# A 32-image, seven-stage pipeline of four residual blocks on one core: setup shared out among the engines, last steps reordered, VectorE's list shortened, two channel masks made by ScalarE

## The chip, the core and the metric

The kernel runs on one core of a Trainium2 chip. The core has five engines with a queue of instructions each: TensorE (PE in the profile; PEld is its loading of weights), VectorE (DVE), ScalarE (ACT), GpSimd (POOL) and SyncE (SP), which here only issues transfers. The engines wait for each other through semaphores. The metric is device time in microseconds (us) of one execution; lower is better.

## The reference, cut to what matters

The input `x` has 32 images of 256 channels and 28 by 28 pixels. Four blocks follow one another, each of them `x = x + block(groupnorm(x))`, with 32 groups of 8 channels:

```
pooled = x.mean(axis=(2, 3)); g = sparsemax(pooled @ gate_w.T + gate_b)
out = einsum('boi,bihw->bohw', einsum('bk,koi->boi', g, expert_w), x)
...
h = prune(relu(bn(depthwise3x3(x) + dw_b)), 4.0)
out = prune(relu(bn(conv1x1(h) + pw_b)), 0.001)
...
q, k, v = split(xt @ Wqkv + bqkv); q = q - mean(q); k = k - mean(k)
k2n = normed(k*k / sum(k*k)) over tokens; q2n = normed(q*q / sum(q*q)) over channels
out = (v + q2n @ (k2n.T @ v) / sqrt(784)) @ Wln + bln
...
out = box3x3(x) / 9
```

`prune` sets a whole channel of an image to zero where its largest value is under the threshold. Since the values come out of a ReLU, "largest value at least the threshold" is the same as "the sum of relu(value - just under the threshold) is above zero". That sum is `h_over` or `y_over`, and the 0 or 1 of each channel is `hmask` or `ymask`.

## The kernel before, in words

The 256 channels are two halves (`j` or `J` = 2) of 128 partitions with 784 columns. The images go through seven stages, and each step `t` (from -1 to 36) works on seven neighbouring images at once: Z = t+1 is loaded, squared and split into a high and a low part; A = t goes through the gate (`gate_logits`, `sparsemax`), the mix of experts (`mix_experts`, `scaled_mix`, `mixed_low`) and the first convolution (`mixed_conv`, `make_x1`); B = t-1 through the depthwise convolution (`first_tap` on ScalarE, then 16 taps of `depthwise` on VectorE, eight per half); C_ = t-2 through the masks and the pointwise convolution (`relu_h`, `sum_over_h`, `h_high`, `h_low`, `pointwise`, `relu_y`, `sum_over_y`, `make_x2`); D = t-3 through the squares of queries and keys and their norms (`square_k`, `square_q`, `fourth_powers_q`, `q_norms`, `q_scales`, `scale_q`, `keys_x`, `kx_low`); E = t-4 through the attention output (`key_rows`, `key_norms`, `value_out`, `attention_out`, `make_x3`); F = t-5 through the box filter. For most images the box is two row sums on VectorE (`box_row_sums`) and three accumulating transfers issued by GpSimd (`add_rows`); for the last two images (TAIL, "in_tail") it is ten additions on VectorE (`box_in_tail`) and a store.

A stage is left out where its image does not exist, so the first steps (images come in) and the last ones (from t = 32, where A is gone) do only part of the work. Steps 8 to 29 are a loop of two steps each; the others are written out.

Each engine's order is the order of the calls in its own `step` (PE L663, DVE L1031, ACT L1328, POOL L1455); nothing else schedules. A step begins with one matmul that makes the group means of all four layers (`group_means`, L488, at the end of PE's list); VectorE reads them (`gn_avg`, L780), makes variances (L786), ScalarE takes the roots (L1114), VectorE makes `gn_r` and `gn_s` (L792, L794) and then the rows `k_rows` (L967). PE has `value_out` of half 0, then waits for these rows in `key_norms` (L540).

Setup: VectorE centres the bias row of queries and keys and splits it in three (L724 to L734) before its first `gn_avg`, does the folded batch-norm constants and the query and key weights at t = 0 (L743 to L756, `parts_of` L715), and the other weights at the end of t = 1 (`setup_weights`, L715 to L772). PE has the weight products at t = 1 (`setup`, L444 to L455).

The two masks are VectorE's, L869 and L883:

```
dve.wait_ge(h_over_sum.sem, h_over_sum.at(C_))
nc.vector.tensor_scalar(hmask[:], h_over[:], 0.0, None, ALU.is_gt).then_inc(hmask_step.sem, 1)
```

## Time and profile before

| what | us |
|---|---|
| median of 3 executions | 1546.27 (1545.89 to 1547.4) |
| the profiled execution, its own time | 1547.11 |
| its span, first to last instruction | 1545.4 |
| PE busy, matmuls | 1404.6 (91%) |
| DVE busy | 1389.4 (90%) |
| ACT busy | 1277.0 (83%) |
| POOL busy | 312.1 (20%) |
| steps 5 to 31, 27 of them, from group means to group means | 1188.14, or 44.01 each |
| from the first instruction to the fourth step's group means (t = -1 to 2) | 107.8 |
| steps 32 to 36 | 161.9 |

The granted clock is TensorE's: 1.00 in the tables is 2.4 GHz and 0.50 is 1.2 GHz, and a stretch with both has a value between. The profile's row of slices shows it at full speed through nearly all of the span, and lower in the first four slices and at the end. A time read from a timeline row is the start of that group and how long it lasted; what stands in brackets is how long the engine was idle before, and what ended that.

### The profile page before, as it was taken

What the parts mean: (1) busy time and instruction counts of PE and PEld (TensorE: products, weight loads), DVE (VectorE), ACT (ScalarE), POOL (GpSimd) and SP (SyncE); (2) the same over time, 40 slices, a digit from 0 to 9 for tenths busy, and PEclk for the clock granted to TensorE, in tenths of its full rate; (3) what the DMA queues carried; (4) which work ended last, traced back from release to release, by engine and by line L of the source; (5) the groups of instructions that cost most, each with busy time, mean ns of one, the idle gap of its engine ahead of it and who ended that gap; (6) DMA issues with size and microseconds to landing.
All of it is one profiled execution on the core that took longest, in us unless ns stands there. A gap on an engine that the chain in (4) does not pass through costs nothing. (4 is left out here: it accounts for less than half of the span.)

```text
span 1545.4 us, 28737 instructions
## 1 busy us (share of the span) xinstructions
PE 1404.6 (91%) x9538; PEld 1246.2 (81%) x9538; DVE 1389.4 (90%) x2553; ACT 1277.0 (83%) x2569; POOL 312.1 (20%) x232
## 2 busy tenths in 40 slices
PE   3449999999999999999999999999999999999983
PEld 2338988888889888888888888888888888888872
DVE  5788899999999999999999999999999999998547
ACT  3268898888899988888999888889998888987852
POOL 2220112222222121211221122212212222111000
PEclk9769999999999999999999999999999999999987
DMA  4100134434443444344443433444434344344431
GB/s 136 41 21 22 38 69 95 94 85 86 103 104 85 81 97 90 84 91 94 104 88 78 101 86 86 99 85 104 93 73 104 83 91 97 64 84 84 84 63 42
DMA packets 45575, 127.92 MB, mean 83 GB/s; under 512 B 3793, under 2 KB 4817, under 8 KB 45522
## 3 DMA queue, kind: packets, MB, share of 16 engines
q0 software_dynamic: 24480, 72.26, 28.1%
q1 hardware_dynamic: 20946, 54.99, 10.2%
q8 instruction: 29, 0.48, 0.1%
q14 instruction: 24, 0.20, 0.0%
q10 hardware_dynamic: 96, 0.00, 0.0%
HBM read 29.29 MB, written 97.94 MB: 82 GB/s over the span
## 5 line engine op out<-in xcount | busy, mean ns | idle before, releaser
L862 DVE SCALAR_TENSOR_TENSOR h<-xpad,dw_sb,h 128x784 f32<-128x784 f32 x512 | 493.6, 1031 | 0.0
L659 PE MATMUL tile_ps<-k,xT 112*128 112x256 f32 x896 | 204.7, 387 | 0.0
L659 PEld LDWEIGHTS tile_ps<-k,xT 112*128 112x128 f32 x896 | 171.6, 194 | 23.1
L585 PE MATMUL tile_ps<-wqk,xn_parts 128*112 128x256 f32 x1344 | 187.5, 294 | 0.0
L1429 POOL TENSOR_SCALAR xpad<-x,gn_rs 128x784 f32<-128x784 f32 x64 | 87.5, 1373 | 483.3 <-DVE x L921 461.4
L1453 POOL DMA_DIRECT2D out<-row_sums x90 | 108.0, 1200 | 364.7 <-DMA out<-row_sums 216.4
L1440 POOL TENSOR_TENSOR x_parts<-x,x_parts 128x784 fp32r<-128x784 f32 x64 | 112.3, 1772 | 339.3 <-ACT x_parts L1180 339.3
L1120 ACT ACTIVATE junk<-x 128x784 bf16<-128x784 f32 x192 | 163.5, 860 | 15.2 <-DVE x L887 4.8
L585 PEld LDWEIGHTS tile_ps<-wqk,xn_parts 128*112 128x112 f32 x1344 | 170.1, 176 | 0.1
L646 PE MATMUL conv_ps<-x_parts,mixed_parts 128*128 128x392 f32 (+1 forms) x768 | 150.6, 353 | 7.4 <-DVE mixed_parts L901 7.4
L504 PE MATMUL conv_ps<-xn_parts,w_out 128*128 128x392 f32 x768 | 152.3, 347 | 0.0
L646 PEld LDWEIGHTS conv_ps<-x_parts,mixed_parts 128*128 128x128 f32 x768 | 140.9, 194 | 10.2 <-issue 10.2
L504 PE MATMUL conv_ps<-hq_parts,pw_parts 128*128 128x392 f32 x768 | 146.1, 346 | 0.0
L504 PE MATMUL conv_ps<-xn_parts,wqk 128*128 128x392 f32 x768 | 142.6, 341 | 0.0
L504 PE MATMUL conv_ps<-hq_parts,attn_parts 128*128 128x392 f32 x768 | 142.4, 341 | 0.0
L504 PEld LDWEIGHTS conv_ps<-hq_parts,pw_parts 128*128 128x128 f32 x768 | 136.4, 189 | 1.7 <-DVE hq_parts L875 1.7
L504 PEld LDWEIGHTS conv_ps<-hq_parts,attn_parts 128*128 128x128 f32 x768 | 137.2, 188 | 0.4 <-DVE attn_parts L980 0.4
L504 PEld LDWEIGHTS conv_ps<-xn_parts,wqk 128*128 128x128 f32 x768 | 135.6, 188 | 0.0
L504 PEld LDWEIGHTS conv_ps<-xn_parts,w_out 128*128 128x128 f32 x768 | 133.4, 188 | 0.0
L1199 ACT ACTIVATE xT<-tile_ps,k_rec 112x256 f32<-112x256 f32 x224 | 89.4, 525 | 0.3 <-PE tile_ps L518 0.3
L1294 ACT ACTIVATE k<-tile_ps 112x256 f32<-112x256 f32 x224 | 83.2, 390 | 4.2 <-PE tile_ps L585 4.2
L631 PE MATMUL small_ps<-expert_sb,mix_w 128*32 128x512 f32 x512 | 66.7, 641 | 8.2 <-DVE mix_w L851 8.2
(162 smaller groups left out, 2748.0 us busy)
## 6 DMA issues: line engine op xcount, KB each, us to landing
out<-row_sums POOLq DMA_DIRECT2D x90, 784.0 KB, 7.1
x<-x SPq DMA_DIRECT2D x32, 784.0 KB, 4.4
out<-x SPq DMA_DIRECT2D x30, 784.0 KB, 3.5
expert_sb<-expert_rows SPq DMA_DIRECT2D x8, 256.0 KB, 5.1
out<-x SPq DMA_DIRECT2D x4, 392.0 KB, 2.4
x<-w_qk SPq DMA_DIRECT2D x1, 512.0 KB, 3.8
x<-w_vT SPq DMA_DIRECT2D x1, 256.0 KB, 7.5
x<-w_ln SPq DMA_DIRECT2D x1, 256.0 KB, 7.5
```

The lines of the kernel that those rows point to most:

```text
L504: mm = nc.tensor.matmul(conv_ps[:, 2 * j + a, 0:HALF], wt[:, half(j)], act[:, a * HALF:(a + 1) * HALF], start=(first and i == 0), stop=(la ...
L585: mm = nc.tensor.matmul(dst, xn2_parts[:, u, i, m * TOK:(m + 1) * TOK], wqk[:, v, i, C:2 * C], start=False, stop=(i == J - 1 and u == 1))
L631: mm = nc.tensor.matmul(small_ps[s * SUB:(s + 1) * SUB, :], mix_w[:, g, :], expert_sb[:, g, s, :], start=(g == 0), stop=(g == PACKED - 1), ...
L646: mm = nc.tensor.matmul(conv_ps[:, 2 * j + a, 0:width], mixed_parts[:, u, i * C + j * P:i * C + (j + 1) * P], x0_parts[:, v, i, a * HALF:a ...
L659: mm = nc.tensor.matmul(tile_ps[:, KX_BANK, i * C:(i + 1) * C], xT[:, m, half(i)], k2[:, m, :], start=(m == 0), stop=(m == M - 1))
L862: nc.vector.scalar_tensor_tensor(acc, view, scalar, acc, ALU.mult, ALU.add).then_inc(dw_step[j].sem, 1)
L1120: nc.scalar.activation(junk[:, j * HW:(j + 1) * HW], source[:, j, :], ACT.Square, accum_out=gn_in[:, layer, 2 + j:3 + j]).then_inc(gn_sums ...
L1199: nc.scalar.activation(xT[:, m, :], tile_ps[0:TOK, XT_BANK[m // 2], m % 2 * C:(m % 2 + 1) * C], ACT.Identity, scale=k_rec[:, m:m + 1]).the ...
L1294: nc.scalar.activation(k2[:, m, :], tile_ps[0:TOK, K_BANK[m // 2], m % 2 * C:(m % 2 + 1) * C], ACT.Square, accum_out=k_sum[:, m:m + 1]).th ...
L1429: nc.gpsimd.tensor_scalar(xpad[:, j, 1:1 + H, 1:1 + W], x1[:, B.odd, j, :].rearrange("p (h w) -> p h w", w=W), gn_r[:, 1, j:j + 1], gn_s[: ...
L1440: nc.gpsimd.tensor_tensor(x0_parts[:, 1, j, 0:HW], x0[:, Z.odd, j, :], x0_parts[:, 0, j, 0:HW].bitcast(F32), ALU.subtract).then_inc(x0_lo. ...
L1453: pool.dma_start(out_dram[F.times(1)], rows, accum_op=ALU.add).then_inc(rows_added[n].of(F), 16)
```

## The change

All of it is order or place of small instructions; no large one is added or taken away.

1. **Masks.** `hmask` and `ymask` are made by ScalarE, as Sign of the two sums, directly behind `sum_over_h` and `sum_over_y`. VectorE's two comparisons go.
2. **VectorE's list, each step.** The sparsemax is written by ranks (two instructions fewer, one reduction over twice the elements); `box_scale` and `mean_lows` go to GpSimd; the square of `k_rec` goes to ScalarE; the limit on the query norm is folded into the two instructions behind the reciprocal; the first gate product is made between variance and reciprocal (`centred_sums`). GpSimd's `normalise_x1` waits for `xn2_lo` in place of `x3_ready`.
3. **Setup.** The bias row is centred and split by ScalarE and GpSimd; ScalarE does the query and key weights at t = 0 but for their low part; PE makes the output weights at t = 0 and VectorE splits them there. The rest of the setup is made at t = 2. ScalarE has its first tap ahead of the sums at t = 1 and 2, and VectorE takes three taps ahead of `mixed_low` there and, at t = 1, seven behind `make_x1`. The first activation is a Sqrt in place of a Square.
4. **Last steps.** Where A is gone, each half of the queries is squared twice at once, the sums of fourth powers go to another PSUM bank and stand ahead of the second half of `pointwise`, and VectorE takes 8 taps ahead of `q_scales`. In the last two steps the box additions of image 30 stand between the other instructions, and `normalise_x3` of a tail image comes early.

```
@@ VectorE, each step
+            def centred_sums(A):
+                dve.wait_ge(gn_read.sem, gn_read.at(A))
+                nc.vector.scalar_tensor_tensor(pooled[:, 0, :], gn_in[:, 0, 0:2], 1.0 / HW, gn_avg[:, 0, 0:2], ALU.mult,
+                                               ALU.subtract).then_inc(gate_step.sem, 1)
...
-                nc.vector.tensor_scalar(zz[:, 1], zz[:, 0], 0.0, None, ALU.max).then_inc(s.sem, 1)
+                nc.vector.tensor_tensor(zz[:, 1], zz[:, 0], z[:].unsqueeze(1).to_broadcast([P, EXPERTS, EXPERTS]),
+                                        ALU.mult).then_inc(s.sem, 1)
...
-                nc.vector.tensor_reduce(excess[:], zz[:, 1], AX.X, ALU.add).then_inc(s.sem, 1)
+                nc.vector.tensor_reduce(upper[:, 0:2, :], zz[:], AX.X, ALU.add).then_inc(s.sem, 1)
...
             def q_scales(D):
                 dve.wait_ge(q_root.sem, q_root.at(D))
-                nc.vector.tensor_scalar(q_alpha[:, 0, :], q_norm[:], NORM_EPS * DIV_EPS, float(HW) ** 0.5, ALU.max,
-                                        ALU.mult).then_inc(alpha_step.sem, 1)
...
+                nc.vector.reciprocal(q_alpha[:], q_norm[:]).then_inc(alpha_step.sem, 1)
...
+                nc.vector.tensor_scalar(alpha_cut, q_alpha[:], ALPHA_MOST, low_row, ALU.min, ALU.mult).then_inc(alpha_step.sem, 1)
@@ ScalarE, the masks
+            def h_mask(C_):
+                act.wait_ge(h_over_sum.sem, h_over_sum.at(C_))
+                if (C_ - 1).active:
+                    act.wait_ge(h_lo.sem, h_lo.at(C_ - 1))
+                nc.scalar.activation(hmask[:], h_over[:], ACT.Sign).then_inc(hmask_step.sem, 1)
+            def y_mask(C_):
...
+                nc.scalar.activation(ymask[:], y_over[:], ACT.Sign).then_inc(ymask_step.sem, 1)
@@ ScalarE, step
+                if F.in_tail:
+                    normalise_x3(F)
...
                 if C_.active:
                     sum_over_h(C_, 0)
                     sum_over_h(C_, 1)
+                    h_mask(C_)
                     h_high(C_)
...
-                if D.active:
-                    square_q(D)
+                if D.active and A.active:
+                    for j in range(J):
+                        square_q(D, j)
                     copy_tokens(D, range(6))
-                    fourth_powers_q(D)
+                    for j in range(J):
+                        fourth_powers_q(D, j)
+                elif D.active:
+                    for j in range(J):
+                        square_q(D, j)
+                        fourth_powers_q(D, j)
+                    copy_tokens(D, range(3))
                 if C_.active:
                     relu_y(C_, 0)
+                    if A.active:
+                        sum_over_y(C_, 0)
+                if D.active:
+                    q_norms(A, D)
+                    if not A.active:
+                        copy_tokens(D, range(3, 6))
+                if C_.active and not A.active:
                     sum_over_y(C_, 0)
-                if D.active:
-                    q_norms(D)
                 if C_.active:
                     relu_y(C_, 1)
                     sum_over_y(C_, 1)
+                    y_mask(C_)
                 if D.active:
                     copy_tokens(D, range(6, M))
                     fourth_powers(D)
@@ TensorE, step
+                if t.number == 0:
+                    setup_output()
                 if D.active:
                     keys(D)
                     queries(D)
                     x2_to_tokens(D, range(3))
                 if C_.active:
-                    pointwise(C_, range(2))
+                    pointwise(C_, range(2 if A.active else 1))
                 if D.active:
-                    query_sums(D)
+                    query_sums(A, D)
+                if C_.active and not A.active:
+                    pointwise(C_, range(1, 2))
@@ VectorE, step
                 if F.in_tail:
-                    box_in_tail(F)
+                    box_in_tail(F, range(5, 7) if E.active else range(10))
                 elif F.active:
                     box_row_sums(F)
+                early = 3 if t.number in (1, 2) else 0
+                if B.active:
+                    depthwise(B, slice(0, early))
...
+                late = 9 if t.number == 1 else 11 if A.active else 8
@@ GpSimd, step
+                if F.active:
+                    box_scale(A, F)
+                if A.active:
+                    mean_lows(A)
+                if t.number == 0:
+                    setup_bias()
                 if B.active:
-                    normalise_x1(A, B, C_, E)
+                    normalise_x1(A, B, C_, D, E)
```

The order of VectorE's instructions in the first full depthwise step (t = 1), before, from the experts' weights on: `mix_w` is the gate's last result, `h<-xpad` are taps, `x,gn_in<-conv_ps` is `make_x1`.

```order
L851 SCALAR_TENSOR_TENSOR mix_w<-gate_own,zeros,mix_const 128x64
L893 TENSOR_TENSOR x_parts<-gn_avg,x_parts 128x2x2
L901 SCALAR_TENSOR_TENSOR mixed_parts<-small_ps,gn_rs,mixed_parts 128x256 x2
L862 SCALAR_TENSOR_TENSOR h<-xpad,dw_sb,h 128x784 x11
L911 SCALAR_TENSOR_TENSOR x,gn_in<-conv_ps,x 128x784 x2
L862 SCALAR_TENSOR_TENSOR h<-xpad,dw_sb,h 128x784 x5
L715 CAST pw_parts<-x 128x512
L716 TENSOR_TENSOR pw_parts<-x,pw_parts 128x512
L715 CAST w_out<-tile_ps 128x512
L716 TENSOR_TENSOR w_out<-tile_ps,w_out 128x512
```

And of the change, the same place, up to the next group means:

```order
L858 SCALAR_TENSOR_TENSOR mix_w<-gate_own,zeros,mix_const 128x64
L869 SCALAR_TENSOR_TENSOR h<-xpad,dw_sb,h 128x784 x3
L893 SCALAR_TENSOR_TENSOR mixed_parts<-small_ps,gn_rs,mixed_parts 128x256 x2
L869 SCALAR_TENSOR_TENSOR h<-xpad,dw_sb,h 128x784 x6
L903 SCALAR_TENSOR_TENSOR x,gn_in<-conv_ps,x 128x784 x2
L869 SCALAR_TENSOR_TENSOR h<-xpad,dw_sb,h 128x784 x7
L793 COPY gn_avg<-small_ps 128x16
```

Three taps now stand ahead of `mixed_low`, and no weight is split in this step.

ScalarE's order in an ordinary step, before, from the roots of the query sums to the last fourth power:

```order
L1319 ACTIVATE q_norm<-tile_ps 128x196
L1284 ACTIVATE x<-conv_ps,bn_shift,bn_scale 128x784
L1276 ACTIVATE over,y_over<-x,below 128x784
L1199 ACTIVATE xT<-tile_ps,k_rec 112x256
L1219 ACTIVATE fourth<-k 112x1792
```

And of the change:

```order
L1371 ACTIVATE q_norm<-tile_ps 128x196
L1338 ACTIVATE x<-conv_ps,bn_shift,bn_scale 128x784
L1330 ACTIVATE over,y_over<-x,below 128x784
L1312 ACTIVATE ymask<-y_over 128x2
L1235 ACTIVATE xT<-tile_ps,k_rec 112x256
L1257 ACTIVATE k_rec<-k_rec 112x7
L1259 ACTIVATE fourth<-k 112x1792
```

The mask of `y` stands between its sum and the next copy, and the square of `k_rec` ahead of the fourth powers; the mask of `h` stands in the same way between its sums and `h_high`.

VectorE's order in step 35, before, from the attention weights on; `row_sums`, `x3pad` and `x<-x,x3pad` are the box additions of image 30:

```order
L980 SCALAR_TENSOR_TENSOR attn_parts<-tile_ps,k_inv,attn_parts 128x256 x2
L921 SCALAR_TENSOR_TENSOR x,gn_in<-conv_ps,b_out,x 128x784 x2
L935 TENSOR_TENSOR row_sums<-x3pad 128x784
L937 TENSOR_TENSOR row_sums<-row_sums,x3pad 128x784
L940 TENSOR_TENSOR x3pad<-row_sums 128x28x28
```

And of the change:

```order
L936 TENSOR_TENSOR row_sums<-x3pad 128x784
L972 SCALAR_TENSOR_TENSOR attn_parts<-tile_ps,k_inv,attn_parts 128x256 x2
L936 TENSOR_TENSOR row_sums<-row_sums,x3pad 128x784
L936 TENSOR_TENSOR x3pad<-row_sums 128x28x28
L913 SCALAR_TENSOR_TENSOR x,gn_in<-conv_ps,b_out,x 128x784
L936 TENSOR_TENSOR x3pad<-x3pad,row_sums 128x28x28
L936 TENSOR_TENSOR x<-x,x3pad 128x784
L913 SCALAR_TENSOR_TENSOR x,gn_in<-conv_ps,b_out,x 128x784
```

Five additions now stand ahead of the last `make_x3`, and one of them ahead of the low part of the attention weights, for which PE waits.

## Rows read from the trace of the kernel before

**Rows 1.** The page: the span in 40 slices, tenths.

```profile
PE   3449999999999999999999999999999999999983
PEclk9769999999999999999999999999999999999987
```

**Rows 2.** Busy time by stretch: stretch, its length, each engine's busy us (count), clock, DMA.

```profile
core 0: us, PE busy (x) PEld busy (x) DVE busy (x) ACT busy (x) POOL busy (x), PEclk, DMA share, GB/s
14.34:40.21 25.87, 12.01 (x46) 8.62 (x46) 13.79 (x51) 6.59 (x17) 2.88 (x2) 0.87 0.21 65
40.21:77.03 36.82, 15.84 (x70) 12.85 (x70) 27.94 (x55) 8.12 (x18) 8.58 (x5) 0.70 0.09 30
77.03:111.11 34.08, 15.16 (x70) 11.57 (x70) 29.30 (x51) 19.50 (x36) 6.33 (x4) 0.65 0.07 24
111.11:153.09 41.98, 36.62 (x240) 31.03 (x241) 33.67 (x64) 35.52 (x71) 5.37 (x4) 0.86 0.07 20
195.32:1383.46 1188.14, 1159.88 (x8022) 1034.32 (x8020) 1136.87 (x2080) 1068.25 (x2153) 261.55 (x187) 1.00 0.43 90
1426.53:1467.15 40.62, 37.96 (x255) 34.32 (x253) 21.34 (x39) 32.37 (x64) 3.61 (x3) 0.96 0.42 80
1467.15:1508.17 41.02, 35.34 (x231) 31.12 (x229) 17.40 (x31) 21.76 (x46) 3.61 (x3) 0.88 0.36 59
1508.17:1545.40 37.23, 11.26 (x70) 10.78 (x68) 26.73 (x43) 8.10 (x15) 0.00 (x0) 0.70 0.11 44
```

**Rows 3.** Waits in the 27 steps from 195.32 to 1383.46: total, times, longest.

```profile
ACT gn_sd L1114 <- DVE gn_var L786: 37.9, 27, 1.6
PE tile_ps L540 <- DVE k_rows L967: 28.3, 27, 1.2
```

**Rows 4.** Timeline of one ordinary step (start, length): ScalarE's rows, then VectorE's.

```profile
732.07 1.59 ACT L1233 CAST xn_parts<-xn 128x784 fp32r<-128x784 f32 x2 [0.81 <-PE conv_ps L504]
...
737.85 1.79 ACT L1266 ACTIVATE hq_parts<-h,hmask 128x784 fp32r<-128x784 f32 x2 [0.24 <-DVE hmask L869]
...
755.18 0.32 ACT L1319 ACTIVATE q_norm<-tile_ps 128x196 f32<-128x196 f32 x1
...
755.53 0.26 DVE L1004 TENSOR_SCALAR q_alpha<-q_norm 128x196 f32<-128x196 f32 x1
...
757.88 0.16 DVE L883 TENSOR_SCALAR ymask<-y_over 128x2 f32<-128x2 f32 x1
758.08 1.04 DVE L887 SCALAR_TENSOR_TENSOR x<-x,ymask 128x784 f32<-128x784 f32 x1
...
768.62 0.68 DVE L1028 TENSOR_TENSOR kx_parts<-tile_ps,kx_parts 128x512 fp32r<-128x512 f32 x1
```

**Rows 5.** Timeline of the same step: a GpSimd and a VectorE row that overlap.

```profile
736.75 3.60 POOL L1429 TENSOR_SCALAR xpad<-x,gn_rs 128x784 f32<-128x784 f32 x2 [15.64 <-DVE x L921]
...
739.67 2.31 DVE L955 TENSOR_TENSOR row_sums<-row_sums,x3pad 128x1568 f32<-128x1568 f32 x1
```

**Rows 6.** Timeline of the first steps, t = -1 to 1.

```profile
8.77 1.28 ACT L1096 ACT_TABLE_LOAD   x1
...
20.15 3.64 PE L631 MATMUL small_ps<-expert_sb,mix_w 128*32 128x512 f32 x16 [2.74 <-DVE mix_w L851]
...
29.09 7.02 PE L646 MATMUL conv_ps<-x_parts,mixed_parts 128*128 128x392 f32 x24 [5.30 <-DVE mixed_parts L901]
...
53.97 10.49 DVE L862 SCALAR_TENSOR_TENSOR h<-xpad,dw_sb,h 128x784 f32<-128x784 f32 x11
```

**Rows 7.** Timeline of the last steps, t = 33 to 35.

```profile
1456.93 0.69 PE L613 MATMUL tile_ps<-kx_parts,picks 128*128 128x196 f32 x4 [2.66 <-DVE kx_parts L1015]
...
1492.71 1.53 PE L601 MATMUL tile_ps<-fourth,ones 128*32 128x196 f32 x16 [3.37 <-ACT fourth L1312]
...
1498.13 8.26 PE L659 MATMUL tile_ps<-k,xT 112*128 112x256 f32 x28
...
1520.13 0.97 DVE L935 TENSOR_TENSOR row_sums<-x3pad 128x784 f32<-128x784 f32 x1
```

351 lines of the change are left out of this document (204 added, 147 removed).

## The prediction

> **What bounds the kernel now.** I read the slices of the page first [rows 1]: PE is busy nine tenths or more everywhere but in the first four slices and the last ones. So there are three kernels in one: a start (t = -1 to 3), 27 ordinary steps and more like them, and an end (t = 32 to 36). The busy table by stretch gives each its price [rows 2]. An ordinary step takes 1188.14 / 27 = 44.01 us, with PE busy 1159.88 / 27 = 42.96 and DVE 42.11. The missing 1.05 us of PE is one wait, for `k_rows` in front of L540: 28.3 / 27 = 1.05 [rows 3]. VectorE is the late one: ScalarE waits 37.9 / 27 = 1.4 us for its variance [rows 3].
>
> That looks like a VectorE bound, and the change cuts VectorE's list. But the timeline of one step shows a closed chain through three engines [rows 4]. ScalarE's L1233 starts at 732.07 when PE is through with `value_out`; ScalarE then works without a gap worth naming until `q_norm` ends at 755.18 + 0.32 = 755.50, 23.43 later; VectorE starts `q_alpha` on it at 755.53, and from there to the end of `kx_low` at 768.62 + 0.68 = 769.30 it is 13.77 more; then come the means, `k_rows` and PE's next `value_out`, some 6.7, and L1233 again. 23.43 + 0.03 + 13.77 + 6.7 = 43.9, nearly the whole step. VectorE's own list and this chain are within 0.1 us of each other. **What the chain does not lose, the step does not lose.**
>
> **The ordinary steps, part by part.** A small dependent VectorE instruction costs 0.20 from start to start (757.88 to 758.08), an independent one about 0.08 (estimates from these rows) [rows 4].
> - Ahead of `q_alpha` VectorE loses: the `hmask` comparison with its wait 0.4, `k_rec` squared 0.2, the gate's first product 0.2 (its successor lies under the wait for ScalarE's root), the sparsemax about 0.2 net, `box_scale` and `mean_lows` 0.15. About 1.15. In many steps GpSimd's second `xpad` meets the row sums: two halves take 3.60, and L955 takes 2.31 [rows 5]. The new wait lets `xpad` start about 1 us earlier, ahead of them; I allow 0.5. All this, 1.6 us, ends in a wait for `q_norm`, which ScalarE does not bring earlier. In the chain it is worth nothing.
> - Behind `q_alpha`: its first instruction of 0.26 goes, 0.30 with the gap. Behind the two cuts VectorE wants `ymask`. That now comes from ScalarE, one Sign behind a sum that VectorE had reached just before. So `make_x2` starts some 0.2 earlier, not 0.5.
> - ScalarE gets the Sign of `h` in the chain: about 0.2 for a tiny activation plus two hand-overs to itself, 0.35, against the gap of 0.24 for VectorE's comparison [rows 4]: +0.1. Bounds: 0 where the old gap was longer, +0.3 if a Sign costs as much as the 0.32 of `q_norm`. The Sign of `y` and the square of `k_rec` lie behind `q_norm`, where ScalarE has a wait for PE to give up.
> - GpSimd's two small instructions run in its idle time (15.64 before `xpad` [rows 5]); if GpSimd took 2 us for each they would still be ahead of L1143 and of `mixed_conv`.
>
> Sum: -0.2 +0.1 in the chain, and -0.1 for the steps in which VectorE itself was last (the collision). **-0.2 per step, for 28 steps (t = 4 to 31): -5.6.** Bounds: +0.1 (+3) and -1.05 (-29), the whole of PE's wait.
>
> **The start.** VectorE's first group-mean row is at 14.34, where the next stretch begins [rows 2], because the bias row comes ahead of it, and the second table load of 1.28 and its root stand at 8.77 [rows 6]. Without them it follows PE's first matmul at about 9.5: -4.8.
> - t = 0 (25.87 [rows 2]): the gate to `mix_w` needs about 6 us, PE's mix 3.64 [rows 6]. VectorE's query and key weights no longer stand between mix and `mixed_low` (part of the 5.30 before L646), but PE has `setup_output` there, 1.9 to 3.8 by the clock (an estimate: it has a third to a half of the work of L646). L646 then takes its 7.02 [rows 6], and behind it ScalarE has one sum of squares less, 0.95. 9.5 + 6 + 3.6 + 3.8 + 7.0 + 3.1 = 33.0 for the next `gn_avg` against 40.21: -2.4 on top. Hidden under it: ScalarE's bias chain (some 8 us while it waited for PE) and its weights (5 us under L646). If that cover fails, the mix starts up to 3 us later.
> - t = 1 (36.82): 11 taps began at 53.97, behind `mixed_low` [rows 6], and the weights' splitting came last. Now VectorE has gate 5.5, three taps 3, `mixed_low` 0.9 with up to 1 us of waiting, six taps 5.8, `make_x1` 2, seven taps 6.7: 24.4. -12.4. A tap is 10.49 / 11 = 0.95.
> - t = 2 (34.08): `setup_columns` +1.8, three taps under ScalarE's `h_high`, and no mask ahead of `make_x2`, where VectorE met GpSimd's `x0_low` (I allow 2 us for that meeting): 29.1, -5.0.
> - t = 3 (41.98): PE-bound through keys and queries, and the gate comes 1 us sooner: -1.1.
>
> Sum -25.7, bounds -18 and -31. The largest unknown is TensorE's clock: 0.87, 0.70 and 0.65 in these stretches [rows 2]. At 1.2 GHz throughout, L646 would take 1 us more in each.
>
> **The end.** In t = 34 PE waits 3.37 for the fourth powers [rows 7]; interleaved with the squares they end about 2.9 sooner. `q_norm` and the shorter q_alpha list follow, with no half clock in L601 (1.53 for what takes 0.9): -4.4. In t = 32 and 33 the wait of 2.66 before L613 [rows 7] seems to be for the taking, but the matmuls behind it need the seventh token copy, which stays behind both sums over `y` and now behind a mask too. I count -0.9 and -0.4. In the last two steps 20 additions of 1 us [rows 7] fill 37.23 [rows 2]. Now seven of image 30's stand in VectorE's waits in t = 35, at a price: `normalise_x3` ahead of `key_norms` on ScalarE, and one addition ahead of `attention_weights_low`, delay `attention_out` by 1.2. The last addition ends 4.7 sooner. Sum **-10.4**, bounds -6 and -14; L659 (8.26) might also get back up to 2 us if the clock does not fall there.
>
> **Total.** -25.7 - 5.6 - 10.4 = -41.7. Span 1545.4 - 41.7 = 1503.7; the profiled execution was 1547.11, so 1505.4, and it was 0.84 over the median: **1504.5**.
>
> **The rivals.**
> - *PE becomes the bound* (0.12). If `q_norm` comes earlier than I think, VectorE's 1.6 us count and PE's wait vanishes: 28 x 1.05 = 29.4 in place of 5.6, 1481. For it: ScalarE waits for PE's `value_out` anyway (0.81). Against it: the 23.4 us of ScalarE behind that wait have no gap, and the change adds to them.
> - *The start and the end give half* (0.13). GpSimd's bias subtractions and `xpad` lock VectorE, the clock stays at 1.2 GHz longer in the denser start, or `attention_out` is later still: -18 and -6 with no gain in the ordinary steps: 1522.
> - *Sign is not in the table of Sqrt* (0.01), slower. Each step has Sqrt, Sign, Sqrt, Sign: four loads of 1.28 [rows 6], three of them in the chain: +3.8 per step, 32 steps +122, less 36: about 1630. It decides from the first t with a mask. Against it: the built program has a single load, where before it had two. The Trainium skill (ScalarE: Activation LUTs, Table sets) does not name sign among the cheap functions that every set has, and puts a switch at about 2.66 us with its drain; by that figure the step would lose twice as much. The row shows 1.28 for the load alone.
> - *The clock falls in the ordinary steps* (0.02), slower. At 1.2 GHz PE's 43 us of a step become up to 86; two such steps cost 86 and eat the gain twice over: 1590. One alone would eat it just. Against it: 1.00 through 1188 us with PE idle 1 us in each step, and the change does not lengthen that.
>
> **How the numbers follow.** Forecast 0.72, with its own range 1493 to 1515; rivals 0.12, 0.13, 0.01, 0.02. The range for 8 in 10 is 1488 to 1520: it leaves out the first rival and the slower ones. Within 0.2% (3 us, what a measurement here can tell) of 1546.3 only a sum of several misses would lie: 0.01. Faster 0.96, slower 0.03.
>
> **What would show it.** After: `gn_avg` first at about 9.5, then 33, 57.4, 86.5, 127; ordinary steps of 43.8 with PE's wait before `key_norms` at 0.8 and not gone; a new wait of VectorE of 1 to 2 us for `q_norm` in each step, and a short one for `ymask`; GpSimd's `xpad` pairs at 2.0; and from the group means of t = 34 to the end 41.02 + 37.23 - 4.4 - 4.7 = 69.1. Wrong would be ordinary steps at 43.0 or over 44.0, a second table load, or a mix that waits for ScalarE's setup at t = 0.

## The result, and the profile after

| | before | after |
|---|---|---|
| median | 1546.84 (4 executions beside these, 1545.89 to 1551.21) | 1521.09 (4, 1519.03 to 1522.42) |
| ratio after / before | | 0.9827, 95% interval 0.9804 to 0.9849 |
| profiled execution, its span | 1547.11, 1545.4 | 1521.87, 1520.2 |
| PE, DVE, ACT, POOL busy | 1404.6, 1389.4, 1277.0, 312.1 | 1400.6, 1346.0, 1300.4, 302.2 |

Faster by 25.8 us, where 41.8 was forecast. The median is 1.1 us above the top of the range (1520), so the prediction was wrong in size and right in direction. VectorE lost 43 us of work, more than the program gained.

The slices of the page, after, against [rows 1]: the same three kernels in one. The second, the third and the last slice are denser.

```profile
PE   3569999999999999999999999999999999999894
PEclk9689999999999999999999999999999999999997
```

The busy table after, by the same stretches as [rows 2] (each begins at a `gn_avg`, where the last four rows of [rows 2] begin at PE's group means, 0.4 to 1.6 earlier; here the ordinary stretch is t = 5 to 31 and t = 32 has a row of its own):

```profile
core 0: us, PE busy (x) PEld busy (x) DVE busy (x) ACT busy (x) POOL busy (x), PEclk, DMA share, GB/s
9.59:33.02 23.43, 11.69 (x54) 7.84 (x54) 14.64 (x41) 14.50 (x40) 6.77 (x7) 0.97 0.47 159
33.02:62.26 29.24, 14.51 (x62) 10.99 (x62) 25.45 (x40) 8.17 (x18) 7.36 (x6) 0.62 0.10 29
62.26:91.31 29.05, 14.12 (x70) 10.70 (x70) 28.05 (x52) 20.10 (x38) 5.71 (x5) 0.73 0.08 28
91.31:131.38 40.07, 35.54 (x240) 29.94 (x241) 32.20 (x57) 35.77 (x74) 5.58 (x5) 0.89 0.07 21
175.08:1366.55 1191.47, 1159.18 (x8018) 1033.55 (x8017) 1108.73 (x1865) 1081.59 (x2233) 249.58 (x241) 1.00 0.44 90
1366.55:1409.22 42.67, 38.63 (x262) 34.51 (x261) 35.40 (x52) 34.49 (x68) 5.84 (x6) 1.00 0.39 76
1409.22:1450.61 41.39, 37.40 (x242) 34.28 (x243) 20.48 (x35) 32.74 (x66) 3.85 (x4) 0.92 0.41 79
1450.61:1488.29 37.68, 34.84 (x230) 31.14 (x230) 16.90 (x29) 21.89 (x47) 3.85 (x4) 0.91 0.39 64
1488.29:1520.20 31.91, 11.23 (x66) 10.48 (x65) 26.12 (x41) 7.65 (x14) 1.06 (x2) 0.73 0.13 51
```

Laid beside the forecast, with the starts of `gn_avg` of both traces (before: t = 4 at 153.09, t = 32 at 1385.07, end 1545.44; after: 131.38, 1366.55, 1520.20):

| part | forecast | measured | off by |
|---|---|---|---|
| start, to `gn_avg` of t = 4 | -25.7 | -21.7 | +4.0 |
| 28 ordinary steps, t = 4 to 31 | -5.6 | 1231.98 to 1235.17: +3.2 | +8.8 |
| end, t = 32 on | -10.4 | 160.37 to 153.65: -6.7 | +3.7 |
| sum | -41.7 | -25.2 | +16.5 |

The three misses are the whole error: 1504.5 + 16.5 = 1521.0. Over half of it is in the ordinary steps, which got longer (44.11 each, against 44.00) although VectorE is busy 28 us less in 27 of them (1108.73 here, 1136.87 in [rows 2]). The waits there, of the stretch 175.08 to 1366.55 (total, times, longest), against [rows 3]:

```profile
ACT gn_sd L1150 <- DVE gn_var L799: 42.3, 27, 1.6
PE tile_ps L554 <- DVE k_rows L959: 32.3, 27, 1.3
DVE k_eps L985 <- ACT k L1348: 19.6, 26, 0.8
DVE q_alpha L996 <- ACT q_norm L1371: 9.4, 27, 0.7
DVE x L885 <- ACT ymask L1312: 5.3, 27, 0.2
```

PE's wait for `k_rows` was to fall from 1.05 to 0.8 a step and rose to 32.3 / 27 = 1.20. VectorE's gain ahead of `q_alpha` did end in waits, as forecast: 19.6 + 9.4 = 29, 1.1 a step, though most of it for the sums of k and not for `q_norm`.

**Where it goes in a step.** One step's timeline after, against [rows 4]: ScalarE, VectorE, GpSimd.

```profile
755.90 1.59 ACT L1273 CAST xn_parts<-xn 128x784 fp32r<-128x784 f32 x2 [0.87 <-PE conv_ps L518]
...
779.13 0.31 ACT L1371 ACTIVATE q_norm<-tile_ps 128x196 f32<-128x196 f32 x1
...
781.53 0.20 ACT L1312 ACTIVATE ymask<-y_over 128x2 f32<-128x2 f32 x1
...
781.99 0.20 ACT L1257 ACTIVATE k_rec<-k_rec 112x7 f32<-112x7 f32 x1
...
779.47 1.38 DVE L996 RECIPROCAL q_alpha<-q_norm 128x196 f32<-128x196 f32 x1 [0.34 <-ACT q_norm L1371]
...
781.76 1.03 DVE L885 SCALAR_TENSOR_TENSOR x<-x,ymask 128x784 f32<-128x784 f32 x1 [0.15 <-ACT ymask L1312]
...
787.58 5.23 DVE L869 SCALAR_TENSOR_TENSOR h<-xpad,dw_sb,h 128x784 f32<-128x784 f32 x5
...
784.80 3.39 POOL L1544 TENSOR_TENSOR x_parts<-x,x_parts 128x784 fp32r<-128x784 f32 x2 [10.05 <-ACT x_parts L1216]
```

From L1273 to the end of `q_norm` it is 23.54, and 23.43 in the step of [rows 4]. That is not the +0.1 of the forecast: in both kernels every second step is 0.1 longer there, and the means over t = 7 to 29 are 23.50 and 23.47. `make_x2` starts 2.29 after `q_alpha` (before 758.08 - 755.53 = 2.55; means 2.33 and 2.55), the forecast -0.2. But the last five taps take 5.23 us; in the step of [rows 4] they took 4.81 (means 5.20 and 4.81). The same group of taps in the form that shows shortest, middle and longest (ns):

```profile
L869 DVE SCALAR_TENSOR_TENSOR h<-xpad,dw_sb,h x5: 1022/1022/1451, 787.6 to 791.8; 128x784 f32<-128x784 f32 x5
```

One of the five, the first, takes 1.45 us and four take 1.02. It starts at 787.58, and GpSimd's two `x0_low` instructions end at 784.80 + 3.39 = 788.19. From t = 7 to 29 one tap in each step is stretched, to 1.42 on average; in the kernel before no tap in the ordinary steps took over 1.04 us. There the taps began at 763.89 and `x0_low` ended at 763.95; from step to step its end lies between 0.20 before and 0.12 after the start of the taps. The change brought them together from both sides. It let the taps start 0.25 sooner after `q_alpha` (8.11, was 8.36) and, by putting the Sign of y and the square of `k_rec` (781.53 and 781.99) on ScalarE ahead of `x0_high`, made `x0_low` start 0.29 later after `q_norm` (5.36, was 5.07).

The row pair of [rows 5] came out as forecast: `xpad` takes 1.98 and L947 1.79 in this step. And only one table load stands in the trace:

```profile
0.87 1.28 ACT L1139 ACT_TABLE_LOAD   x1 [0.87 <-PEq L1632]
```

**The first steps**, against [rows 6]. VectorE in t = 0 (two rows), then GpSimd and VectorE in t = 1:

```profile
10.08 1.50 DVE L799 SCALAR_TENSOR_TENSOR gn_var<-gn_avg,gn_sq 128x8 f32<-128x8 f32 x1
...
16.53 1.24 DVE L858 SCALAR_TENSOR_TENSOR mix_w<-gate_own,zeros,mix_const 128x64 f32<-128x64 f32 x1
...
30.69 3.37 POOL L1544 TENSOR_TENSOR x_parts<-x,x_parts 128x784 fp32r<-128x784 f32 x2 [13.01 <-ACT x_parts L1216]
...
35.71 2.02 POOL L1527 TENSOR_SCALAR xpad<-x,gn_rs 128x784 f32<-128x784 f32 x2 [0.73 <-DVE gate_in L823]
...
52.67 4.10 POOL L1544 TENSOR_TENSOR x_parts<-x,x_parts 128x784 fp32r<-128x784 f32 x2 [14.94 <-ACT x_parts L1216]
...
33.23 0.85 DVE L797 TENSOR_TENSOR gn_sq<-gn_avg 128x8 f32<-128x8 f32 x1
...
37.06 0.74 DVE L837 TENSOR_TENSOR zz<-zz,z 128x64 f32<-128x64 f32 x1
...
44.30 0.88 DVE L893 SCALAR_TENSOR_TENSOR mixed_parts<-small_ps,gn_rs,mixed_parts 128x256 fp32r<-128x256 f32 x2 [1.93 <-ACT mixed_parts L1198]
...
52.69 9.65 DVE L869 SCALAR_TENSOR_TENSOR h<-xpad,dw_sb,h 128x784 f32<-128x784 f32 x7
```

The seven taps take 9.65 where 6.7 was counted, beside an `x0_low` of 4.10. Even two tiny instructions of 0.17 and 0.22 us are stretched to 0.85 and 0.74, and each ends as a GpSimd instruction ends (34.06 and 37.73). So it is in t = 0: the variance takes 1.50 for 0.17 and ends at 11.58, as `x0_low` ends (11.55), and `mix_w` takes 1.24 for 0.28 and ends at 17.77, as the second subtraction of the bias by GpSimd ends (17.68).

**The last steps**, against [rows 7]: the end of t = 32 and the start of t = 33, PE and VectorE, then t = 34.

```profile
1397.78 6.28 PE L676 MATMUL tile_ps<-k,xT 112*128 112x256 f32 x28 [1.90 <-ACT xT L1235]
...
1411.12 0.59 PE L554 MATMUL tile_ps<-norm_weight,k_rows 128*128 128x2 f32 x2 [2.65 <-DVE k_rows L959]
1411.57 1.63 PE L566 MATMUL tile_ps<-w_out,kx_parts 128*128 128x256 f32 x6
...
1397.37 1.03 DVE L885 SCALAR_TENSOR_TENSOR x<-x,ymask 128x784 f32<-128x784 f32 x1 [2.25 <-ACT ymask L1312]
...
1401.05 7.65 DVE L869 SCALAR_TENSOR_TENSOR h<-xpad,dw_sb,h 128x784 f32<-128x784 f32 x8
...
1472.99 0.87 PE L618 MATMUL small_ps<-fourth,ones 128*32 128x196 f32 x16 [0.58 <-ACT fourth L1364]
...
1477.45 8.62 PE L676 MATMUL tile_ps<-k,xT 112*128 112x256 f32 x28
```

The wait for the fourth powers fell from 3.37 to 0.58, as forecast. But in t = 32 VectorE, which first waits 2.25 for `ymask`, has eight taps left and ends last, so PE waits 2.65 for `k_rows`.

### The profile page after: what moved, and what is told of

It is laid out like the page before. It is cut to its first block and busy times, and to the rows that moved or that the text cites. A ratio compares the mean times of both kernels' runs of the same rounds, so it can differ in the third digit from the quotient of the medians.

```text
span 1520.2 us, 28640 instructions
## 1 busy us (share of the span) xinstructions
PE 1400.6 (92%) x9538; PEld 1242.2 (82%) x9538; DVE 1346.0 (89%) x2273; ACT 1300.4 (86%) x2688; POOL 302.2 (20%) x298
## 5 line engine op out<-in xcount | busy, mean ns | idle before, releaser
L869 DVE SCALAR_TENSOR_TENSOR h<-xpad,dw_sb,h 128x784 f32<-128x784 f32 x512 | 506.7, 1055 | 0.0
L676 PE MATMUL tile_ps<-k,xT 112*128 112x256 f32 x896 | 201.7, 383 | 3.8 <-ACT xT L1235 3.8
L676 PEld LDWEIGHTS tile_ps<-k,xT 112*128 112x128 f32 x896 | 169.5, 192 | 26.3 <-issue 4.1
L1544 POOL TENSOR_TENSOR x_parts<-x,x_parts 128x784 fp32r<-128x784 f32 x64 | 109.2, 1723 | 353.1 <-ACT x_parts L1216 353.1
L663 PE MATMUL conv_ps<-x_parts,mixed_parts 128*128 128x392 f32 (+1 forms) x768 | 146.6, 347 | 2.3 <-DVE mixed_parts L893 2.3
L663 PEld LDWEIGHTS conv_ps<-x_parts,mixed_parts 128*128 128x128 f32 x768 | 137.2, 191 | 4.3 <-issue 4.3
L1527 POOL TENSOR_SCALAR xpad<-x,gn_rs 128x784 f32<-128x784 f32 x64 | 63.5, 1001 | 248.7 <-DVE xn_parts L979 205.4
```

The lines of the kernel that those rows point to most:

```text
L663: mm = nc.tensor.matmul(conv_ps[:, 2 * j + a, 0:width], mixed_parts[:, u, i * C + j * P:i * C + (j + 1) * P], x0_parts[:, v, i, a * HALF:a ...
L676: mm = nc.tensor.matmul(tile_ps[:, KX_BANK, i * C:(i + 1) * C], xT[:, m, half(i)], k2[:, m, :], start=(m == 0), stop=(m == M - 1))
L869: nc.vector.scalar_tensor_tensor(acc, view, scalar, acc, ALU.mult, ALU.add).then_inc(dw_step[j].sem, 1)
L1527: nc.gpsimd.tensor_scalar(xpad[:, j, 1:1 + H, 1:1 + W], x1[:, B.odd, j, :].rearrange("p (h w) -> p h w", w=W), gn_r[:, 1, j:j + 1], gn_s[: ...
L1544: nc.gpsimd.tensor_tensor(x0_parts[:, 1, j, 0:HW], x0[:, Z.odd, j, :], x0_parts[:, 0, j, 0:HW].bitcast(F32), ALU.subtract).then_inc(x0_lo. ...
```

## The experiments

Twelve kernels. "Step" is the mean of t = 4 to 30, from one `gn_avg` to the one 27 steps on (before: (1341.22 - 153.09) / 27 = 44.00; after: (1323.31 - 131.38) / 27 = 44.15). Ratios are to the kernel before, measured again beside each run.

| run | median | ratio (95% interval) | step | t = 1 | t = 32, 33, 34 |
|---|---|---|---|---|---|
| before | 1546.84 | | 44.00 | 36.82 | 41.89, 40.63, 41.02 |
| after | 1521.09 | 0.9827 (0.9804 to 0.9849) | 44.15 | 29.24 | 42.67, 41.39, 37.67 |
| short_x0_low | 1504.79 | 0.9726 (0.9710 to 0.9743) | 43.74 | 27.98 | 42.67, 40.32, 36.54 |
| ymask_k2_vector | 1512.59 | 0.9776 (0.9755 to 0.9797) | 43.89 | 29.19 | 42.65, 41.06, 37.73 |
| hmask_vector | 1521.76 | 0.9847 (0.9830 to 0.9864) | 44.15 | 28.23 | 42.65, 40.33, 36.50 |
| before_signs | 1544.92 | 0.9993 (0.9982 to 1.0003) | 44.03 | 36.76 | 43.10, 38.96, 40.26 |
| t32_eleven | 1517.12 | 0.9814 (0.9798 to 0.9831) | 44.16 | 28.80 | 39.85, 40.30, 34.84 |
| drain_copy_first | 1519.83 | 0.9824 (0.9807 to 0.9840) | 44.16 | 29.34 | 43.30, 38.77, 36.53 |
| t1_eleven | 1519.91 | 0.9829 (0.9812 to 0.9845) | 44.15 | 27.85 | 42.68, 38.60, 36.54 |
| combined | 1500.20 | 0.9701 (0.9685 to 0.9717) | 43.54 | 27.89 | 42.72, 36.60, 34.86 |
| x0_high_early | 1510.71 | 0.9763 (0.9748 to 0.9778) | 43.79 | 29.16 | 42.68, 40.30, 37.75 |
| xpad_wait_before | 1522.02 | 0.9837 (0.9822 to 0.9852) | 44.15 | 28.29 | 42.68, 41.36, 37.70 |
| combined_two | 1495.44 | 0.9671 (0.9656 to 0.9687) | 43.54 | 27.97 | 39.45, 36.59, 34.83 |
| combined_no_q_norm | 1507.27 | 0.9743 (0.9728 to 0.9758) | 43.91 | 27.87 | 40.86, 36.62, 36.52 |

### Take the meeting away

```diff
                     pool.wait_ge(x0_hi.sem, x0_hi.at(Z, j + 1))
...
-                    nc.gpsimd.tensor_tensor(x0_parts[:, 1, j, 0:HW], x0[:, Z.odd, j, :], ...
+                    n = 8 if j and Z.number != 0 else HW
+                    nc.gpsimd.tensor_tensor(x0_parts[:, 1, j, 0:n], x0[:, Z.odd, j, 0:n], ...
```

> The changed kernel, but GpSimd's second x0_low instruction (channel half 1) subtracts 8 of its 784 columns, from image 1 on; the other 776 columns keep old data, so that part of the computation is left out. Nothing else differs. Theory (the taps meet GpSimd): in the changed kernel the first of the last five taps takes 1.38 to 1.45 us where the others take 1.02, because it starts before GpSimd's second x0_low has ended. Without that the first tap is 1.02, ordinary steps go from 44.18 to 43.8 us (28 x 0.4 = 11), t = 1 loses the second stretched tap only, about 1.3 us of 3, t = 2 and 3 some 1.5 together: about 1507 us, ratio 0.974 to the kernel before. Rival 1 (the two Signs and their hand-overs on ScalarE are what lengthened the steps): no change, 1521, steps of 44.18. Rival 2 (a stretched tap is only slack that the step then spends waiting elsewhere): the tap falls to 1.02 and the step stays at 44.1 or more.

This kernel leaves out most of GpSimd's second subtraction, so its time is a measurement and not a gain. Measured: 1504.79, forecast 1507. GpSimd ends before the taps, and all five are alike:

```profile
732.16 2.02 POOL L1545 TENSOR_TENSOR x_parts<-x,x_parts 128x784 fp32r<-128x784 f32 x2 [10.00 <-ACT x_parts L1216]
...
L869 DVE SCALAR_TENSOR_TENSOR h<-xpad,dw_sb,h x5: 1026/1026/1028, 735.0 to 738.8; 128x784 f32<-128x784 f32 x5
```

The step fell by 0.41, what the tap had been stretched by (1.42 - 1.02 = 0.40). Both rivals fall: the Signs are still on ScalarE here, and no other wait took the 0.4.

### Give operations back to VectorE

```diff
+                dve.wait_ge(y_over_sum.sem, y_over_sum.at(C_))
+                nc.vector.tensor_scalar(ymask[:], y_over[:], 0.0, None, ALU.is_gt).then_inc(ymask_step.sem, 1)
                 dve.wait_ge(ymask_step.sem, ymask_step.at(C_))
...
+                nc.vector.tensor_tensor(k_rec2[:], k_rec[:], k_rec[:], ALU.mult).then_inc(rec2_ready.sem, 1)
...
-                nc.scalar.activation(k_rec2[:], k_rec[:], ACT.Square).then_inc(rec2_ready.sem, 1)
...
-                    y_mask(C_)
```

> The changed kernel with two tiny operations given back to VectorE: the mask of y (one comparison) and the square of k_rec. ScalarE then reaches x0_high 0.30 us sooner after q_norm (0.20 + 0.10), and GpSimd's x0_low ends 0.3 sooner, while VectorE's make_x2 starts no later, since it had waited 0.15 for the Sign of y. Theory (the taps meet GpSimd): the first of the last five taps falls from 1.42 to about 1.15, ordinary steps from 44.18 to 43.9, total 1521 - 28 x 0.27 = 1513. Rival 1 (ScalarE's Signs cost in the chain by themselves, wherever x0_low lies): the Sign of y lies behind q_norm, so nothing or at most 0.05 a step: 1520. Rival 2 (VectorE is the bound again, so 0.4 us more on it lengthens the step): 44.5, 1530.

Measured: 1512.59, forecast 1513; steps of 43.89, forecast 43.9. The stretched tap takes 1.09 on average. VectorE does 0.4 us more in each step and the step is 0.26 shorter.

```diff
+            def h_mask(C_):
...
+                nc.vector.tensor_scalar(hmask[:], h_over[:], 0.0, None, ALU.is_gt).then_inc(hmask_step.sem, 1)
...
-                    h_mask(C_)
                     h_high(C_)
```

> The changed kernel with the mask of h alone given back to VectorE, ahead of the row sums. Theory (the chain ScalarE to q_norm to VectorE, plus the meeting of tap and x0_low): from the release of ScalarE by PE's value_out to q_norm 0.1 us less (23.54 to 23.43), and the meeting stays as it is, so steps of 44.08 and 1518. The 0.4 us that VectorE spends for it falls in its waits for the sums of k and for q_norm (0.80 and 0.34). Rival (VectorE's list is the bound): steps of 44.4 or more, 1528.

Measured: 1521.76 and steps of 44.15, no change at all, where 44.08 was forecast. From L1273 to `q_norm` it is 23.48 on average, 23.50 with the Sign on ScalarE: the 0.1 that I had charged to the Sign of h is 0.02. It also shows that 0.4 us more on VectorE ahead of `q_alpha` cost nothing.

### The masks alone, in the kernel before

```diff
-                nc.vector.tensor_scalar(hmask[:], h_over[:], 0.0, None, ALU.is_gt).then_inc(hmask_step.sem, 1)
...
-                nc.vector.tensor_scalar(ymask[:], y_over[:], 0.0, None, ALU.is_gt).then_inc(ymask_step.sem, 1)
...
+                nc.scalar.activation(hmask[:], h_over[:], ACT.Sign).then_inc(hmask_step.sem, 1)
...
+                nc.scalar.activation(ymask[:], y_over[:], ACT.Sign).then_inc(ymask_step.sem, 1)
```

> The kernel before with the masks alone changed: both are made by ScalarE as signs of its sums. No other part of the change. Theory: the Sign of h adds 0.1 to the chain; VectorE's make_x2 starts up to 0.2 earlier and x0_low ends 0.2 later, so they meet the last five taps: before, x0_low ended 0.06 us after the first of them had started and its time was not seen to be longer; now the overlap is 0.4 and the first tap takes 1.2 to 1.35. Ordinary steps go from 44.02 to about 44.15, 28 x 0.13 = 3.6, 1550, ratio 1.002. Rival 1 (my forecast of the masks: +0.1 in the chain, -0.5 + 0.3 behind q_alpha): steps of 43.9, 1543, ratio 0.998. Rival 2 (the table of Sqrt lacks Sign): four loads a step, 1660; the trace of the changed kernel speaks against it.

Measured: ratio 0.9993 with 1 in its interval, steps of 44.03 against 44.00. Between the two forecasts (44.15 and 43.9), so as a forecast of size both missed. The meeting is there: `make_x2` starts 0.19 sooner after `q_alpha` (2.36), and the first of the last taps takes 1.29 to 1.38. One eats the other. The two masks by ScalarE, alone, are worth nothing.

### GpSimd earlier instead of smaller

```diff
                     copy_tokens(D, range(6, M))
+                    if Z.active:
+                        x0_high(Z)
                     fourth_powers(D)
...
-                if Z.active:
+                if Z.active and not D.active:
                     x0_high(Z)
```

> The changed kernel with one move on ScalarE: x0_high ahead of the fourth powers of k (1.69 us), in the steps with both. Signs, lists and waits as in the changed kernel. x0_high must wait for PE's mixed convolution (L663, ending 3.7 us after q_norm), so its first half comes about 0.85 us sooner and GpSimd's x0_low starts at some 4.55 after q_norm (5.36 in the changed kernel) and ends at 7.9 to 8.0, before the last five taps start at 8.1. Theory (a tap waits for GpSimd's running instruction, nothing else is wrong with the step): no tap over 1.05 us, steps fall from 44.18 to 43.8 as in the run without half of x0_low, total about 1507. Rival 1 (it is the load that x0_low puts on the step, wherever it stands): another VectorE instruction is stretched by 0.4 instead and the step stays at 44.18. Rival 2 (the fourth powers, now 1.9 later, make PE wait before the second half of the key sums): PE's L545 is late, steps of 44.2 or more.

Measured: 1510.71, steps of 43.79, forecast 1507 and 43.8. The full `x0_low` now ends as the taps start:

```profile
735.64 3.39 POOL L1546 TENSOR_TENSOR x_parts<-x,x_parts 128x784 fp32r<-128x784 f32 x2 [9.80 <-ACT x_parts L1216]
...
738.82 4.82 DVE L869 SCALAR_TENSOR_TENSOR h<-xpad,dw_sb,h 128x784 f32<-128x784 f32 x5
```

It is the same work on every engine as in the changed kernel, 0.36 a step cheaper by its place. Neither rival showed. Here 0.21 of `x0_low` lies beside the tap and costs it nothing. Laid side by side, the ordinary steps of all traces give one relation: where `x0_low` ends 0.2 us or less after the start of the first of the last taps, that tap takes its 1.03; where it ends 0.25 after, 1.08; 0.31, 1.15; 0.46, 1.29; 0.55, 1.38; 0.62, 1.45. The delay is the overlap less 0.2.

### VectorE's time ahead of q_alpha

```diff
-                if D.active:
+                if D.active and not E.active:
                     pool.wait_ge(xn2_lo.sem, xn2_lo.at(D))
```

> The changed kernel with GpSimd's xpad waiting for the end of x3, as in the kernel before, and not for the low half of x2. Theory: xpad meets the row sums again (pairs of 3.60 us, row sums of 2.3 or 2.5 in place of 1.79), VectorE loses 0.5 to 0.7 ahead of q_alpha, and this ends in its waits for the sums of k and for q_norm (0.80 and 0.34): ordinary steps as in the changed kernel, 44.15 to 44.25, total 1521. Rival (what VectorE loses ahead of q_alpha counts): steps of 44.7, 1535.

Measured: 1522.02 and steps of 44.15. The collision of [rows 5] is back and costs VectorE 0.7:

```profile
759.30 3.51 POOL L1527 TENSOR_SCALAR xpad<-x,gn_rs 128x784 f32<-128x784 f32 x2 [9.26 <-DVE x L913]
...
761.97 2.48 DVE L947 TENSOR_TENSOR row_sums<-row_sums,x3pad 128x1568 f32<-128x1568 f32 x1
```

`k_eps` (L985), which had waited 0.8 for ScalarE, starts in this step without a wait, and the step is the same to 0.01. A collision of 0.7 where VectorE has slack costs nothing, and one of 0.4 where it is in the chain costs all of it.

### t = 1 and the last steps

```diff
-                late = 9 if t.number == 1 else 11 if A.active else 8
+                late = 11 if t.number == 1 else 11 if A.active else 8
```

> The changed kernel with eleven taps ahead of make_x1 in t = 1, not nine. In the changed kernel make_x1 ends as GpSimd's x0_low begins (52.67 to 56.77), and the two taps that meet it take 2.66 and 2.34 us in place of 1.02; in ordinary steps x0_low runs beside make_x1 and scale_q, which read PSUM, and costs nothing there. Theory (a tap is held while GpSimd runs x0_low, an instruction that reads PSUM is not): with make_x1 at 52.7 to 54.6 the first half of x0_low is free, the second stretches one tap by 1.3 to 1.5 us: t = 1 falls from 29.24 to 27.7, total 1519.5. Rival (any VectorE work beside x0_low is slowed): make_x1 is stretched instead, t = 1 stays at 29.2 and the total at 1521.

Measured: t = 1 in 27.85, forecast 27.7; the total, 1519.91, is too near to tell. `x0_low` begins as `make_x1` does:

```profile
52.74 3.38 POOL L1544 TENSOR_TENSOR x_parts<-x,x_parts 128x784 fp32r<-128x784 f32 x2 [15.00 <-ACT x_parts L1216]
...
52.67 1.03 DVE L903 SCALAR_TENSOR_TENSOR x<-conv_ps,x 128x784 f32<-128x784 f32 x1
...
54.59 6.16 DVE L869 SCALAR_TENSOR_TENSOR h<-xpad,dw_sb,h 128x784 f32<-128x784 f32 x5
```

Both `make_x1` instructions (one input in PSUM) keep their 1.03, and one tap takes 2.38, ending 1.35 late, while 56.12 - 54.59 = 1.53 of GpSimd's second half was left. The runs whose t = 1 is as in the changed kernel took 28.2 to 29.3. The two shortest of them (hmask_vector 28.23, xpad_wait_before 28.29) have the same order, but there `x0_low` happened to begin 1.5 before the seven taps, and the two taps that meet it take 1.18 and 2.34. So what the move of two taps is worth lies between 0.4 and 1.5; that the meeting sets the length of t = 1, these executions show as well.

```diff
-                late = 9 if t.number == 1 else 11 if A.active else 8
+                late = 9 if t.number == 1 else 11
```

> The changed kernel with one number of VectorE's list as in the kernel before: in t = 32 eleven of the sixteen taps stand ahead of q_alpha, not eight. In the changed kernel VectorE waits 1.45 for q_norm and 2.25 for ymask there and has eight taps (7.65 us) left behind scale_q, so it ends t = 32 last (gn_avg 2.4 after PE's group means), k_rows is 2.65 late for PE, and PE's next matmuls run at half clock (L566 1.63 us for 0.96, L518 3.56 for 2.39). Theory: the three taps fill the waits; t = 32 falls from 42.67 to 40.1, and t = 33 from 41.39 to 39.4 since PE no longer waits and keeps its clock: 4.6 us, 1516.5. Rival (the later q_alpha delays PE's scales and keys_x by as much): L676 waits for the seventh token copy at 1397.8 anyway, q_alpha would have to be over 2 us later; then 1521. Ordinary steps as in the changed kernel, 44.18.

Measured: 1517.12, forecast 1516.5. t = 32 took 39.85 (forecast 40.1), and PE no longer waited for `k_rows` (the first L566 back at 0.96); t = 33 took 40.30 for the 39.4 forecast: PE waited there 1.90 for the seventh token copy, and L676 behind that wait took 7.97 for 6.28.

```diff
                 if C_.active and not A.active:
                     sum_over_y(C_, 0)
+                if D.active and not A.active:
+                    copy_tokens(D, range(6, M))
```

> The changed kernel with ScalarE's seventh token copy, in the last steps only, ahead of relu_y 1, of the second sum over y and of the Sign of y. In the changed kernel PE's L676 waits 1.90 for that copy in t = 32 and again in t = 33. Theory: in t = 33, where PE is last, 1.9 us go (41.39 to 39.5); in t = 32 nothing, since there VectorE's eight taps are last; 1519. Rival (the wait moves on to relu_y 1 and make_x2, now 0.5 later): t = 33 unchanged, 1521.

Measured: 1519.83, forecast 1519, within the spread of the total. t = 33 took 38.77 (forecast 39.5) and t = 32, where `make_x2` comes later and VectorE is last, 43.30, 0.6 more. PE's L676 followed its scales at once. But t = 33 moves by itself: 38.60 to 41.39 in the seven traces whose last steps are the changed kernel's but for the place of the masks and of `k_rec2`. The granted clock moves with it: 1.00 in the row of 38.60, 0.96 in the three of 40.30 to 40.33, 0.92 in the three of 41.06 to 41.39. In the changed kernel the row of t = 33 has a clock of 0.92, and L566 takes 1.63 behind the wait for `k_rows`; in t1_eleven the same instructions follow the same wait of 2.65:

```profile
1407.69:1446.30 38.61, 34.61 (x242) 31.37 (x243) 20.49 (x36) 32.63 (x66) 3.85 (x4) 1.00 0.44 84
...
1409.60 0.38 PE L554 MATMUL tile_ps<-norm_weight,k_rows 128*128 128x2 f32 x2 [2.65 <-DVE k_rows L959]
1409.84 0.96 PE L566 MATMUL tile_ps<-w_out,kx_parts 128*128 128x256 f32 x6
```

Here PE stayed at 2.4 GHz; there it ran at 1.2 GHz behind the wait, and the step is 2.8 us longer. The row of t = 33 in drain_copy_first has the low clock too, and must be held against 41.39:

```profile
1411.60:1450.37 38.77, 36.67 (x242) 33.70 (x243) 20.49 (x35) 32.85 (x66) 3.85 (x4) 0.91 0.41 78
```

At like clocks the copy is worth 2.6 in t = 33. In the kernels below, with all these moves, t = 33 takes 36.6.

### Put together

The masks of y and the square on VectorE, the two numbers of `late`, the early copy, and in all steps with A:

```diff
                 if C_.active:
                     relu_y(C_, 0)
-                    if A.active:
-                        sum_over_y(C_, 0)
...
-                if C_.active and not A.active:
+                if C_.active:
                     sum_over_y(C_, 0)
...
+                if B.active and t.number not in (1, 2, 3):
+                    upto = 12 if A.active else 2 * TAPS - 2
+                    depthwise(B, slice(late, upto))
+                    late = upto
                 if C_.active:
                     make_x2(C_)
```

> The changed kernel with what the runs so far point to: the mask of y and the square of k_rec on VectorE; q_norm on ScalarE ahead of the first sum over y in all steps, as soon as PE's L618 is done; one tap (in t = 32 five) moved ahead of make_x2 to fill the wait for ymask; eleven taps ahead of q_alpha or make_x1 in t = 1 and t = 32; the seventh token copy first in the last steps. Theory: q_alpha starts 0.34 sooner (then VectorE's taps are what it waits for), the moved tap covers the later ymask, and the last four taps start after x0_low has all but ended: ordinary steps 43.4 to 43.5, 28 x 0.7 = 20; t = 1 to 3 about 3; the end 6: about 1491, ratio 0.964. Rival 1 (the chain has another part of equal length behind it, PE's 42.9 plus k_rows): steps no shorter than the 43.79 of the run without half of x0_low, 28 x 0.4 = 11: 1500. Rival 2 (ScalarE's idle time ahead of q_norm is lost to it and it becomes the bound): steps of 44.1, 1511.

Measured: 1500.20, forecast 1491. The total is that of rival 1, but its steps of 43.79 did not come: they took 43.54, a little above the 43.4 to 43.5 expected. t = 32 gained nothing: five taps ahead of `make_x2` and `scale_q` held PE up, which waits for `scale_q`, and what followed ran at half clock (0.85 us is its usual time):

```profile
1387.97 1.24 PE L545 MATMUL tile_ps<-k,k_rec 112*32 112x256 f32 x11 [1.85 <-DVE q L1014]
```

```diff
-                    upto = 12 if A.active else 2 * TAPS - 2
+                    upto = 12
```

> The kernel of the run named combined with one change: in t = 32 one tap, not five, stands ahead of make_x2. In combined, PE waited there 1.85 for scale_q behind the five taps (L545), and 3.38 us passed on VectorE until PE's group means at half clock. Theory: t = 32 falls from 42.72 to 40, the rest as in combined (steps 43.58): 1497.5. Rival (the clock falls there for another reason, the wait for q_alpha's scales): 42.7 as it is, 1500.

Measured: 1495.44, forecast 1497.5; t = 32 in 39.45. By the ratios it is 1.6% faster than the changed kernel and 3.3% faster than the one before. Its ordinary step:

```profile
726.40 1.38 DVE L1000 RECIPROCAL q_alpha<-q_norm 128x196 f32<-128x196 f32 x1
...
735.41 3.87 DVE L869 SCALAR_TENSOR_TENSOR h<-xpad,dw_sb,h 128x784 f32<-128x784 f32 x4
...
732.07 3.39 POOL L1541 TENSOR_TENSOR x_parts<-x,x_parts 128x784 fp32r<-128x784 f32 x2 [10.40 <-ACT x_parts L1224]
```

`q_alpha` waits for nothing, one tap (at 728.45) lies where the wait for the mask would be, and GpSimd ends at 735.46, as the last four taps start.

The same without the two moves around `q_norm`:

> The kernel of combined_two without its two moves in the ordinary steps (q_norm ahead of the first sum over y, and the tap ahead of make_x2); kept are the mask of y and the square of k_rec on VectorE, eleven taps in t = 1 and 32, and the seventh token copy first in the last steps. Theory: the parts add up: ordinary steps 43.91 as in the run with these two operations alone, so 0.33 x 28 = 9 more than combined_two: about 1506.5. Rival (q_norm's place is worth nothing and the missing meeting alone makes combined faster): steps of 43.6, 1498.

Measured: 1507.27, forecast 1506.5; steps of 43.91. So `q_norm`'s place (with its tap) is worth 0.37 a step, and the parts add up.

## Why the prediction was wrong

**The ordinary steps.** The step that failed is the line "Behind `q_alpha`", where I followed VectorE's list as if the durations of its instructions were fixed. The chain itself was right. Taken apart by the traces (means of t = 7 to 29, after less before): the wait from `q_norm` to `q_alpha` -0.08, from `q_alpha` to `make_x2` -0.22, ScalarE up to `q_norm` +0.03, the last taps +0.39, all the rest +0.04. Against the forecast of -0.1, -0.2, +0.1 and nothing for the taps, three terms are right or nearly so; the Sign of h was priced too high. Without the meeting the steps gain 0.26 (43.74 in short_x0_low) where -0.2 was forecast. What was missing is where two lists meet. I had asked what the Sign of y and the square of `k_rec` do to ScalarE ("behind `q_norm`, where ScalarE has a wait for PE to give up") and not who starts on ScalarE's next result: GpSimd, whose `x0_low` ends where the taps begin. Both ends stood in the trace of the kernel before (760.57 + 3.38 = 763.95 and 763.89), in two lists that I had not laid side by side. It cost 28 x 0.40 = 11 us, more than the 8.8 by which this part was off. Steps over 44.0 were among the prediction's own signs of being wrong.

That GpSimd and VectorE hold each other up I knew and used elsewhere: for `xpad` and the row sums [rows 5], for t = 2, and as part of the rival that start and end give half. The Trainium skill (SBUF — State Buffer, Who interferes with whom) states it: a VectorE instruction with two SBUF inputs and a GpSimd instruction that reads SBUF shut each other out for whole instructions, and one with at most one SBUF input, outside the modes that use both port pairs, is free. The traces here agree that the first kind is held (a tap ends 0.43 late for an overlap of 0.61) and the second is not (`make_x1` with one input in PSUM takes 1.03 beside `x0_low`). By that rule of the Trainium skill the delay would be the whole overlap; measured, it is 0.2 less. That the mutual exclusion is by a port that the two share is the Trainium skill's statement; the runs show only who is held and for how long.

**The start.** t = -1 and 2 came out as forecast (-4.8 and -5.0), t = 3 a little better (-1.9 for -1.1). The total of t = 0 did too (-2.4), but by luck: from `gn_avg` to the end of `mix_w` it is 8.2 for the 6 counted, with the variance and `mix_w` held by GpSimd, the second by the very bias subtractions that the rival names; ScalarE, with the weights in its list, worked without a gap from 21.66 to 32.19 and PE's group means waited for it, so the end took 4.8 for 3.1; and against that L663, at full clock, took 4.58 for the 7.0 counted, and what stands between mix and L663 took 2.2 for 3.8. What did hold is that the mix did not wait for ScalarE.

All of the miss is in t = 1: 29.24 for 24.4. The terms of the forecast give 23.9 and "up to 1 us of waiting", so the sum had half of that. Measured: seven taps 9.65 for 6.7 (+2.9); the gate up to the first tap 39.45 - 33.02 = 6.4 for 5.5 (+0.9, where the two tiny instructions are held for 1.2 together); the wait ahead of `mixed_low` 1.93 (+1.4); the other terms 0.4 less. The first two are the same meeting: in short_x0_low, where the first tiny one is not held, the gate takes 5.75, and t1_eleven with one tap held took 27.85 where 27.7 was forecast. Why the wait was longer, no run was made to show.

**The last steps.** The last two steps gave -4.9 for -4.7. The step that failed is t = 32, +0.8 for -0.9. Not seen was VectorE: with eight taps ahead of `q_alpha`, not eleven, t = 32 ends on VectorE. The description of the change names the eight taps (its point 4); the prediction priced PE's chain alone and never asked what VectorE had left behind `q_alpha`. It cost 42.67 - 39.85 = 2.8 us (t32_eleven). The seventh copy kept PE waiting 1.90, which I had seen; it is what became of the 2.66 of [rows 7].

t = 33 (+0.8 for -0.4) and t = 34 (-3.35 for -4.4) were off by the clock of this one execution as much as by the forecast. Where the row of t = 33 has a clock of 0.96, as before the change, it took 40.30 to 40.33, which is -0.3; where the row of t = 34 has 0.95, it took 36.50 to 36.54, which is -4.5. In t = 34 of the profiled execution `q_norm` came 3.4 sooner, but L676 stayed slow, 8.62 for the 8.26 of before, where t32_eleven, with a granted clock of 1.00 in that stretch, had 6.23 and a t = 34 of 34.84. That the late `k_rows` makes the clock fall is not shown: t1_eleven kept 1.00 behind the same wait, and t32_eleven, without it, fell later in the step.

**What held.** What VectorE loses ahead of `q_alpha` is worth little more than nothing (0.08 a step in all; giving parts of it back in hmask_vector and xpad_wait_before changed nothing, to 0.01); a single table load; `xpad` pairs at 2.0; from PE's group means of t = 34 to the end 70.0, forecast 69.1. PE did not become the bound. The case measured is by its total the rival "the start and the end give half" (1522), but not by its mechanism: there the ordinary steps gain nothing, here they lost 3, and start and end gave 28 of 36. Part of that rival's mechanism was there, though: GpSimd's bias subtractions did hold VectorE in t = 0.

## What to carry to other kernels

When a change shortens one engine's list, or puts work ahead of something on a second engine, lay the lists of all engines of the stretch side by side and look for pairs that end and begin within a few tenths of a microsecond; between GpSimd and VectorE such a pair is a price of its own, and it shows in no wait, only in the longest duration of a group. Compare means over many steps before calling a tenth of a microsecond the effect of a change: here odd and even steps differ by as much. Place a GpSimd instruction beside VectorE instructions that read PSUM, or where VectorE waits anyway: the same 0.4 to 0.7 us cost everything in one place and nothing in another. After moving work behind a wait, add up what is left behind it: the last steps of a pipeline have another last engine than the full ones.

## What the runs showed of the hardware

- A VectorE instruction held up by GpSimd has no idle time before it in the profile: it starts on time and lasts longer (1.45 us for 1.02; 0.85 for 0.17). Tiny ones end within 0.1 us of GpSimd's end (33.23 + 0.85 = 34.08 and 34.06; 37.06 + 0.74 = 37.80 and 37.73; 16.53 + 1.24 = 17.77 and 17.68). A tap is held by the overlap less 0.2 us, in the ordinary steps of every trace; up to 0.2 us costs nothing.
- It goes both ways: in t = 1 of the changed kernel GpSimd's two `x0_low` took 4.10 us (1.84 and 2.30) beside two taps of 2.66 and 2.34; in t1_eleven, where the first ran beside `make_x1` and the second began just before the tap, they took 3.38 (1.85 and 1.57).
- Sign on ScalarE takes 0.20 us for two columns and needed no other table than Sqrt's (one load of 1.28 us in the whole trace); a chain of sum, Sign and use on ScalarE was no slower than with VectorE's comparison in between (44.15 either way).
- The same wait of PE, 2.65 us, was followed by 1.2 GHz in one execution and by 2.4 GHz in another of the same instructions: 41.39 and 38.61 us for the same step.
